# Blocks of 128 rows made of two 64-row pieces of any two of 64 small experts

## The reference

```python
logits = jnp.einsum('bsh,he->bse', hidden_states.astype(jnp.float32), router_w)
affinity = jax.nn.sigmoid(logits)
top_scores, top_idx = jax.lax.top_k(affinity, K)          # K = 8 of E = 64
gate_out = jnp.einsum('bsh,ehi->bsei', hidden_states, expert_gate_k)   # h 256, i 128
up_out = jnp.einsum('bsh,ehi->bsei', hidden_states, expert_up_k)
expert_act = jax.nn.silu(gate_out) * up_out
routed = jnp.einsum('bsei,eih->bsh', expert_act * router_mask[..., None], expert_down_k)
```

## Time and profile before

| | us |
|---|---|
| median of 3 runs | 2946.24 (2945.65 to 2948.47) |
| the profiled execution | 2942.13 |
| its span, first to last instruction | 2940.4 |
| the blocks stage, from TensorE's first transpose to ScalarE's last copy of y | 1425.9 to 1729.8 |

### The profile page before, as it was taken

How to read it: one execution, slowest core, us unless ns; L and a number is a source line. 1 busy time by engine, 2 the same in 40 slices (tenths; PEclk the granted TensorE clock), 3 DMA queues, 4 the chain that set the end, 5 groups by cost and what they waited for, 6 DMA issues and landing times. The chain is left out here.

```text
span 2940.4 us, 58466 instructions
## 1 busy us (share of the span) xinstructions
PE 2799.0 (95%) x17307; PEld 1928.4 (66%) x17308; DVE 1525.5 (52%) x4471; ACT 1029.3 (35%) x2709; POOL 926.6 (32%) x1784
## 2 busy tenths in 40 slices
PE   7999999999999999995999988999999999999798
PEld 5777676677777677674788855556565665656475
DVE  4445555555555555554655545555555555554343
ACT  1433334333433434332333323343333433334121
POOL 0012222122112222113455535534344343430332
PEclk9999999999999999997999999999999999999899
DMA  6000000000000000002588871100001000000350
GB/s 224 8 7 7 7 7 7 7 7 2 7 5 7 7 7 7 7 2 93 157 264 260 197 166 30 40 24 21 21 25 34 24 21 21 28 17 4 122 187 20
DMA packets 89488, 154.78 MB, mean 53 GB/s; under 512 B 19266, under 2 KB 64335, under 8 KB 87888
## 3 DMA queue, kind: packets, MB, share of 16 engines
q1 hardware_dynamic: 39952, 85.60, 9.0%
q0 software_dynamic: 22320, 45.30, 6.5%
q10 hardware_dynamic: 27152, 23.09, 2.3%
HBM read 122.86 MB, written 31.99 MB: 53 GB/s over the span
## 5 line engine op out<-in xcount | busy, mean ns | idle before, releaser
L927 PE MATMUL psG<-W,ctxT 128*125 128x512 f32 (+2 forms) x896 | 408.6, 599 | 4.2 <-DVE v L2435 4.2
L1520 ACT ACTIVATE probs<-psG,nmax 112x375 f32<-112x375 f32 (+1 forms) x512 | 317.0, 620 | 252.0 <-DVE nmax L1891 252.0
L921 PE MATMUL psG<-ctxT,W 128*128 128x375 f32 (+1 forms) x1024 | 386.8, 525 | 2.3 <-ACT ctxT L1718 1.2
L1891 DVE TENSOR_REDUCE nmax<-psG 112x1 f32<-112x375 f32 (+1 forms) x512 | 284.9, 601 | 120.5 <-PE psG L869 116.0
L886 PEld LDWEIGHTS psT<-ident,probs 112*125 112x125 f32 (+2 forms) x1792 | 201.3, 167 | 157.5 <-ACT probs L1520 110.6
L921 PEld LDWEIGHTS psG<-ctxT,W 128*128 128x128 f32 x1024 | 188.9, 189 | 163.1 <-issue 106.5
L915 PEld LDWEIGHTS psG<-hT,W 128*128 128x128 f32 x2304 | 268.5, 194 | 24.9 <-ACT hT L1547 16.2
L915 PE MATMUL psG<-hT,W 128*128 128x112 f32 x2304 | 278.9, 280 | 3.2 <-ACT hT L1547 3.2
L927 PEld LDWEIGHTS psG<-W,ctxT 128*125 128x125 f32 (+2 forms) x896 | 159.6, 187 | 177.9 <-issue 170.8
L886 PE MATMUL psT<-ident,probs 112*125 112x112 f32 (+2 forms) x1792 | 248.5, 276 | 20.2 <-ACT probs L1520 16.3
L869 PE MATMUL psG<-kT,qT 64*112 64x375 f32 (+1 forms) x1024 | 243.9, 563 | 1.1 <-DVE v L2435 0.6
(11 more groups left out here) (374 smaller groups left out, 4190.8 us busy)
## 6 DMA issues: line engine op xcount, KB each, us to landing
W<-in_ew SPq DMA_DIRECT2D x64, 384.0 KB, 4.6
expert_rows<-W ACTq DMA_DIRECT2D x176, 128.0 KB
W<-in_ew SPq DMA_DIRECT2D x8, 2048.0 KB, 8.9
ctxT<-in_ctxT SPq DMA_DIRECT2D x16, 375.0 KB, 3.1
kT<-in_ctx SPq DMA_DIRECT2D x16, 375.0 KB
W<-in_eb SPq DMA_DIRECT2D x8, 640.0 KB, 10.9
normed_rows<-hrow SPq DMA_DIRECT2D x32, 112.0 KB, 1.9
W<-normed_rows,ids POOLq DMA_INDIRECT x176
```

What stands on the lines that cost most here:

```text
L921: mm = nc.tensor.matmul(bank[:, 0:n], wt[:, c, n0 + j * P:n0 + (j + 1) * P], src[:, c, 0:n], start=(c == 0), stop=(c == DC - 1))
L927: mm = nc.tensor.matmul(bank[0:kn, 0:512], src[:, c, k0:k0 + kn], wt[:, c, n0 + half * 512:n0 + (half + 1) * 512], start=(c == 0), stop=(c ...
L1520: nc.scalar.activation(probs[:, 2 * (s % 2) + i, 0:keys], psG[0:T, score_banks(s)[i], 0:keys], ACT.Exp, bias=nmax[:, h:h + 1], accum_out=r ...
L1891: nc.vector.tensor_reduce(nmax[:, 2 * s + i:2 * s + i + 1], psG[0:T, score_banks(s)[i], 0:keys], AXX, ALU.max, negate=True).then_inc(max_r ...
```

## The change

For the 64 small experts a block is made of two pieces of 64 rows, and the two pieces may belong to any two experts. The eight large experts keep blocks of 128.

- `Experts` gets a piece size. There are at most 14336/64 + 64 = 288 pieces, so 144 blocks. `brow` has 288 entries, one for each piece, and the tables count in pieces (add 63, shift by 6). The id rows of 64 numbers are fetched by four indirect loads. `lrow` is halved to blocks at the end.
- TensorE multiplies each half of the rows with its own weights: the upper piece (rows 0 to 63) with the weights in the ring, the lower piece (rows 64 to 127) with weights at a fixed place, `lower[i]`, one of eight. Each product becomes two, with 64 stationary columns each, into PSUM partitions 0 to 63 and 64 to 127.
- The weights of the lower piece are copied there from the ring for every block: ScalarE copies gate and up (512 elements of each partition), VectorE copies down (256). Each reads the rank of the lower piece from `brow` into a register, computes the place in the ring, and waits until that rank is loaded. This is so too where both pieces are of one expert.
- The pipelines of TensorE, ScalarE and VectorE go in pairs of blocks. On TensorE: transposes of blocks i and i+1, transposes of h of i-4 and i-3, gate and up of i-2 and i-1, down of i-4 and i-3. `xT0` gets four buffers for two.
- Some semaphores are shared between the two mixtures, and `brow` moves to the storage of `hT1` and `hT2`.

```diff
-        self.NBLK = -(-(TOK * topk // P + experts) // 4) * 4
+        self.NBLK = -(-(TOK * topk // piece + experts) * piece // P // 4) * 4
+        self.NP = self.NBLK * P // piece
...
-        L0E, L1E = Experts(0, 64, 8, 8, 768), Experts(1, 8, 1, 4, 5376)
+        L0E, L1E = Experts(0, 64, 8, 8, 768, 64), Experts(1, 8, 1, 4, 5376, P)
...
+        lower = [W[:, 17152 + 768 * i:17920 + 768 * i] for i in range(5)]
+        lower += [flat[:, 512 + 768 * i:1280 + 768 * i] for i in range(3)]
...
             for i, n in enumerate((P, L0E.NBLK - P)):
-                nc.gpsimd.indirect_dma_start(
-                    out=idrow[0:n, i, :], out_offset=None, in_=rows0,
-                    in_offset=bass.IndirectOffsetOnAxis(ap=gcol[0:n, i:i + 1], axis=0)).then_inc(S0.idrow_in, 16)
+                for k in range(2):
+                    nc.gpsimd.indirect_dma_start(
+                        out=idrow[0:n, i, half * k:half * k + half], out_offset=None, in_=rows0,
+                        in_offset=bass.IndirectOffsetOnAxis(ap=gcol[0:n, 2 * i + k:2 * i + k + 1],
+                                                            axis=0)).then_inc(S0.idrow_in, 16)
...
+                def pair(turn, i, lo, hi=0):
+
                     if hi < 1:
...
+                        for k in range(i, i + 2):
+                            j = At(turn, k, UNROLL)
+                            pe.wait_ge(s.xg_in[j.m], 16 * (j.turn + 1))
+                            for c in range(DC):
+                                mm = nc.tensor.transpose(psG[:, j.m2, c * P:(c + 1) * P], xg0[:, j.m, c * P:(c + 1) * P],
+                                                         ident[:])
+                            mm.then_inc(s.xT_full, 1)
+                    if lo >= 2:
+                        for k in range(i - 4, i - 2):
+                            j = At(turn, k, UNROLL)
+                            pe.wait_ge(s.h_done, j.j + 1)
+                            nc.tensor.transpose(psT[:, j.m2, 0:P], hh[:, j.m2, :], ident[:]).then_inc(s.hT_full, 1)
                     if lo >= 1 and hi < 2:
...
+                        for k in range(i - 2, i):
+                            j = At(turn, k, UNROLL)
+                            pe.wait_ge(s.xT_done, j.j + 1)
+                            pe.wait_ge(s.loaded, pe.snap(first[k % 4], min_val=0, max_val=l.E - 1) + 1)
+                            pe.wait_ge(s.up_copied, j.j + 1)
+                            for c in range(DC):
+                                for h in range(2):
+                                    mm = nc.tensor.matmul(psG[half * h:half * h + half, 2 + j.m2, 0:256],
+                                                          xT0[:, j.m, c, half * h:half * h + half], weights(c, k, h),
+                                                          start=(c == 0), stop=(c == DC - 1))
+                            mm.then_inc(s.gu_full, 1)
...
+                            pe.wait_ge(s.hT_done, j.j + 1)
+                            pe.wait_ge(s.down_copied, j.j + 1)
+                            if not (isinstance(j.j, int) and j.j < 2):
+                                pe.wait_ge(s.y_done, j.j - 1)
+                            for h in range(2):
+                                mm = nc.tensor.matmul(psO[half * h:half * h + half, j.m2, 0:D],
+                                                      hhT[:, j.m2, half * h:half * h + half], weights(2, k, h),
+                                                      start=True, stop=True)
+                            mm.then_inc(s.y_full, 1)
...
+                def copy_up(j, i):
+
+                    act.reg_load(loaded_rank, brow[0:1, bass.ds(2 * j + 1, 1)])
+                    act.reg_alu(rank, loaded_rank, 0, ALU.max)
+                    act.reg_alu(slot, rank, l.R - 1, ALU.bitwise_and)
+                    act.reg_alu(slot, slot, l.wsize, ALU.mult)
+                    act.wait_ge(s.loaded, act.snap(rank, min_val=0, max_val=l.E - 1) + 1)
+                    at = act.snap(slot, min_val=0, max_val=(l.R - 1) * l.wsize)
+                    nc.scalar.activation(lower[i][:, 0:512], W[:, bass.ds(RING + at, 512)],
+                                         ACT.Copy).then_inc(s.up_copied, 1)
+
+                def pair(turn, i, lo, hi=0):
+                    if hi < 1:
+                        for k in range(i, i + 2):
+                            copy_up(At(turn, k, UNROLL).j, k)
                     if lo >= 1 and hi < 2:
...
+                        for k in range(i - 2, i):
+                            j = At(turn, k, UNROLL)
+                            act.wait_ge(s.gu_full, j.j + 1)
+                            nc.scalar.activation(sg[:, j.m2, :], psG[:, 2 + j.m2, 0:P], ACT.Silu).then_inc(s.sg_done, 1)
+                    if lo >= 2:
+                        for k in range(i - 4, i - 2):
+                            j = At(turn, k, UNROLL)
+                            act.wait_ge(s.y_full, j.j + 2)
+                            act.wait_ge(s.y_stored[j.m], 16 * j.turn + 16)
+                            nc.scalar.activation(ysb0[:, j.m, :], psO[:, j.m2, 0:D], ACT.Copy).then_inc(s.y_done, 1)
+                            act.wait_ge(s.y_done, j.j + 1)
+                            store(l, s, j)
```

More of the change, by code:

```diff
@@ L1206, in tables1 @@
                 pe.wait_ge(s.slots_ok, B)
[L1207 removed]
+                nc.tensor.matmul(psG[0:E, 0, 0:1], cum1, ones[0:T, 0:1], start=True, stop=True).then_inc(S0.counts_full, 1)
                 pe.wait_ge(s.blocks_ok, 1)
@@ L1240, in blocks0 @@
                 pe.sem_inc(s.y_full, 1)
[L1242 to L1248, removed]
-                    if hi < 1:
[L1250 to L1255, removed]
-                    if lo >= 1 and hi < 2:
[L1257 to L1274, removed]
@@ new lines, in blocks0, with weights @@
+                half = l.piece
+                first = [pe.alloc_register(f"upper_rank{i}") for i in range(4)]
+                slots = [pe.alloc_register(f"ring_slot{i}") for i in range(UNROLL)]
+                def weights(c, i, k):
+                    if k:
+                        return lower[i % UNROLL][:, 256 * c:256 * c + 256]
+                    slot = pe.snap(slots[i % UNROLL], min_val=0, max_val=(l.R - 1) * l.wsize)
+                    return W[:, bass.ds(RING + slot + 256 * c, 256)]
@@ L1275, in step @@
                     if hi < 1:
-                        load_rank(At(turn, i, UNROLL).j, i, l)
-                for i in range(UNROLL):
-                    step(0, i, i)
+                        for k in range(i, i + 2):
+                            load_upper(At(turn, k, UNROLL).j, k)
+                for i in range(0, UNROLL, 2):
+                    pair(0, i, i // 2)
                 with pe.Fori(1, l.NBLK // UNROLL) as turn:
-                    for i in range(UNROLL):
-                        step(turn, i, 3)
@@ L1283, in blocks0 @@
-                for i in range(3):
-                    step(l.NBLK // UNROLL, i, 3, i + 1)
+                    for i in range(0, UNROLL, 2):
+                        pair(turn, i, 2)
+                for i in range(0, 4, 2):
+                    pair(l.NBLK // UNROLL, i, 2, i // 2 + 1)
             def blocks1(l, s):
@@ L1664, in blocks0 @@
[L1664 to L1670, removed]
+                act.wait_ge(s.tables, 1)
+                loaded_rank = act.alloc_register("loaded_rank_act")
+                rank, slot = act.alloc_register("lower_rank_act"), act.alloc_register("lower_slot_act")
@@ L1672, in blocks1 @@
+                for i in range(0, UNROLL, 2):
+                    pair(0, i, i // 2)
+                with act.Fori(1, l.NBLK // UNROLL) as turn:
+                    for i in range(0, UNROLL, 2):
+                        pair(turn, i, 2)
+                for i in range(0, 4, 2):
+                    pair(l.NBLK // UNROLL, i, 2, i // 2 + 1)
             def blocks1(l, s):
@@ L2280, in blocks0 @@
-                for i in range(4):
-                    step(0, i, i)
-                with dve.Fori(1, l.NBLK // 4) as turn:
-                    for i in range(4):
-                        step(turn, i, 4)
-                for i in range(2):
-                    step(l.NBLK // 4, i, 4, i + 1)
+                dve.wait_ge(s.tables, 1)
+                loaded_rank = dve.alloc_register("loaded_rank_dve")
+                rank, slot = dve.alloc_register("lower_rank_dve"), dve.alloc_register("lower_slot_dve")
@@ new lines, in pair @@
+                def pair(turn, i, lo, hi=0):
+                    if hi < 1:
+                        for k in range(i, i + 2):
+                            j = At(turn, k, UNROLL)
+                            dve.wait_ge(s.xT_full, j.j + 1)
+                            nc.vector.tensor_copy(xT0[:, j.m], psG[:, j.m2, 0:DC * P].rearrange(
+                                "p (c t) -> p c t", c=DC)).then_inc(s.xT_done, 1)
+                    if lo >= 2:
+                        for k in range(i - 4, i - 2):
```

(19 more changed lines are left out.)

164 lines of the change are left out of this document (86 added, 78 removed).

## The result

| | before | after |
|---|---|---|
| median | 2946.91 us (2945.65 to 2948.47, 4 runs) | 2971.59 us (2969.18 to 2973.50, 4 runs) |
| the profiled execution; its span | 2942.13; 2940.4 | 2972.38; 2970.6 |
| ScalarE's last copy of y ends at | 1729.83 | 1756.18 |

The ratio is 1.0085, with an interval from 1.0072 to 1.0097: 25 us slower.

What follows compares the result with a forecast made beforehand. TensorE bounds the kernel before; after the change ScalarE's 4.30 us lap would bound the small experts' stage. Stage +7.7 and tables +3.0 give +10.7 us, a median of 2957 us from 2946.24, range 2926 to 2990.

Steps and rivals of the forecast that it cites:

- the plain lap: ScalarE's work for one pair of blocks, with every wait on others satisfied: 4.30 us.
- Part 1 and 3: Small experts: 144 blocks for 176 save TensorE 53 us; VectorE with its weight copies needs 3.4 to 3.7 us a pair.
- Part 2: Products in halves on TensorE: halves run side by side, 0.25 us for mode changes, 3.51 us a pair against 3.32.
- Part 4: Weight copies on ScalarE: its lap becomes 4.30 us a pair against TensorE's 3.51, so ScalarE becomes the bound.
- register part: ScalarE's rank read, address and wait value ahead of each weight copy: 0.72 us, twice a pair, the first exposed behind a store.
- weights come late: Rival: copies or products wait for expert weights to arrive, each us of wait one of the end; chance 0.03.
- The Trainium skill's rule on SBUF copies: ScalarE's SBUF copies: latency exposed between instructions would remove the 0.10 us overlap, result 7 us later; one copy 0.61 us.
- Stage in sum: Small experts' stage: second SiLU at 1432.4, 69 laps of 4.30, end at 1737.5 against 1729.8, so +7.7 us.
- Part 5: Tables and id rows: two more indirect loads +2.5 us, wider comparisons and one more shift +0.5.
- TensorE as the bound: Rival: ScalarE's reads hide and the lap falls to TensorE's 3.51 us, giving 2902 us; chance 0.24.
- The halves in turns: Rival: TensorE's half products run one after another, 6.1 us a pair, +135 us, 3081; chance 0.05.
- a falling clock: Rival: TensorE, partly idle, is held at 1.2 GHz, 6.9 us a pair, +190 us, 3136; chance 0.04.

Runs made afterwards that it cites:

- e1: Changed kernel with ScalarE's weight copies taken from a fixed place, without rank read, register operations or load wait (wrong weights): 2913.11 us, 0.9901 of the kernel before.
- e7: Changed kernel with one y copy and one store for a pair, and ScalarE's ranks read a pair ahead: 2927.01 us, 0.9948 of the kernel before.
- e9: Changed kernel with TensorE's reads of the next pair's ranks between gate/up and down instead of behind down: 3108.37 us, 1.0092 of the kernel before.
- e12: Kernel of e7 with TensorE's rank reads moved between the gate/up and down products: 2954.03 us, 1.0044 of the kernel before.
- e11: Kernel of e7 run again, on one chip with e12: 2925.66 us, 0.9946 of the kernel before.
- e4: Changed kernel with y of a pair copied by one instruction and stored by one DMA: 2934.74 us, 0.9976 of the kernel before.
- e5: Changed kernel with ScalarE's two rank reads for the next pair placed behind this pair's weight copies: 2935.98 us, 0.9990 of the kernel before.

## Why the prediction was right, and its size too small

The sign, the bound and the plain lap were right; the forecast was +10.7 us and the medians say +24.7.

- **Part 1 and 3.** 72 pairs ran. VectorE did not set the pace in the changed kernel: in each pair it waits 1.5 us for SiLU (65.8 us in 44). At 3.70 us a pair (e1) it still kept up, within my 3.4 to 3.7. The row of 0.28 that I took for a copy from SBUF is a product which reads PSUM too; the copies took 0.34 to 0.35 on the average.
- **Part 2, TensorE's pair of 3.51.** Its halves run side by side. In the timeline of TensorE two passes start within 0.01 us, and the next two 0.21 later:

```profile
1551.93 0.38 PE L1298 MATMUL psG<-W 128*64 x1
1551.94 0.38 PE L1298 MATMUL psG<-kT,W 128*64 128x256 f32 x1
1552.14 0.38 PE L1298 MATMUL psG<-W 128*64 x1
1552.15 0.38 PE L1298 MATMUL psG<-kT,W 128*64 128x256 f32 x1
```

  The first half product starts at 1551.67 and the second pair at 1551.93, so 0.05 more than a pitch, where 0.25 was charged for going in and out of the halves. What the part left out is TensorE's own reads, two ahead of each pair with nothing queued behind the down products: 27.2 us of 200, and 39.6 in e7. It did not cost the changed kernel anything (e9). I took it for what stops e7 at 3.92 instead of 3.51; but with these reads moved the kernel was slower (e12), so what holds e7 there is not shown.
- **Part 4, the lap of 4.30.** The plain laps are 4.31 (only the first two, at 4.19 and 4.18, are shorter). The register part behind a store was 0.79 (read 0.27, the rest 0.52) and the hidden one 0.77 from copy to copy, each for 0.72; the stores were as charged; the two SiLUs with their wait values took 0.32 for 0.43. That 4.31 lies so near is in part luck: these two errors cancel. But 69 laps, from the first copy of y at 1437.64 to the one at 1749.83, took 312.2 us, 4.52 each, where 296.7 stood in the sum. **This is the term that was too small:** the lap was summed with every read at its median and the branch at next to nothing. Of the 15.5 us too few, 2.8 are the plain lap (4.31 for 4.27 without the branch). Another 4.3 are the loop's branch: the 16 laps that hold it are 0.40 longer, 0.31 of that between the store's issue (end 1552.69) and the weight copy and 0.08 ahead of the second copy of y, where I charged 0.03 a lap. The last 8.4 are long reads: the 138 reads of ScalarE's sequencer in these laps took 8.4 us more in sum than at 0.275 each, and in all but three laps the excess over 4.31, the branch aside, is that of the lap's two reads within 0.05 us.
  The rows of line 1703 name the arrival of weights (L463) ahead of ten copies:

```profile
  issue: 101.7, 122
  SPq L463: 11.7, 10
```

  But these ten waited no longer than their own reads explain. A copy behind a store has 1.30 us of idle time, a second one 0.15, with reads of 0.27. Two of the named waits:

```profile
1485.51 0.63 ACT L1703 ACTIVATE W<-W 128x512 f32 x1 [1.41 <-SPq L463]
1576.10 0.63 ACT L1703 ACTIVATE W<-W 128x512 f32 x1 [1.31 <-SPq L463]
```

  The read ahead of the first took 0.38, that of the second 0.29; in none of the ten are more than 0.03 us left over. So "weights come late" did not happen: in all ten the load's signal came 0.07 to 0.93 us before the copy started.
  One sum of the range is incomplete: its lower end, 3.86, takes the register part's bound and not the copy's, with which it would be 3.73.
- **The Trainium skill's rule on SBUF copies.** The 0.10 of overlap was kept: a weight copy ends at 1559.53, and the SiLU behind it starts at 1559.43. In e11 two SBUF copies stand in a queue:

```profile
1557.49 1.15 ACT L1707 ACTIVATE W<-W 128x512 f32 x2 [0.97 <-ACT W L1725]
```

  Two copies in 1.15 us, where one is 0.63: the second starts 0.10 before the end of the first. The Trainium skill, page "VectorE: DVE Perf Modes", section on the TRN2 errata, says that SBUF latency stays exposed between instructions; for ScalarE's copies this trace does not agree, and its length for one (an estimate of 0.61) does.
- **Stage in sum.** The second SiLU ended at 1434.4, where 1432.4 and the tables' 3.0 give 1435.4: 1.0 early. From the first transpose to that SiLU it took 4.5 us where before took 5.1; the two blocks transposed ahead, charged with 1.4, cost nothing. From there to the last y came 321.7 for 305.1: the 15.5 of the laps, and 1.1 in the first lap and the drain. At the stage's end that is +26.3 for +10.7. Behind the stage the profiled execution took 3.8 us more than that of before (1214.4 for 1210.6), which this account leaves open.
- **Part 5.** The wait for the id rows is 1.5 us longer, where I took 2.5; the tables add 1.5 for 0.5 (0.45 of it was there before their first instruction on VectorE). Some 1.2 us more (the conversion of the id rows to floats comes 2.7 later, the first transpose 4.0) are lost in the shared expert, at a granted clock of 0.91 from 1405 to 1425, where before had 1.00; the cause is open.
- **The rivals.** TensorE as the bound needed a lap of 3.5; it came near only with ScalarE's reads away (e1). The halves in turns and a falling clock did not happen: the granted clock was 1.00 with TensorE waiting in every pair.

## What to carry to other kernels

Cut work on the engine that sets the end only after summing the lap of the engine that takes over, its sequencer included: here two parts of 0.8 us, reads and address arithmetic, of which one lay bare behind a store, helped to turn fewer blocks, worth 1.66 to 1.97 us each, into a loss. Then add to that best lap what single laps cost beyond it (the branch, the reads that are longer than their median); here it was 5% of the lap and more than the whole forecast. Where such a loss is found, first take the register reads and stores off the queue that decides: with one store for two blocks and ScalarE's ranks read a pair ahead, e7 and e11 beat both kernels, at 0.9948 and 0.9946 of the one before.

## What the runs showed of the hardware

- A sequencer's read of one integer from SBUF takes 0.27 (ScalarE) to 0.30 us (TensorE, VectorE) at its shortest, and up to 1.17 (e12). With the shorter laps of e11, 125 of 305 were over 0.5 us, against 24 of 264 after. Each of them, and of SyncE's that were as long, overlaps in time with a read of another engine's sequencer (136 in e11, 29 after). Overlap alone doesn't make a read long: 140 of the 250 that took under 0.33 us in e11 overlap too. The gains of e4 and e5, 32 and 30 us, became 39 together; these long reads are a likely cause, and no run took them away.
- A loop's branch made ScalarE's lap 0.40 us longer; the branch instruction itself is 0.045.
- A copy of 512 elements for one of 256 twice, from PSUM, took 0.60 us for 0.77, and the issue of a store of two blocks 0.38 for 0.34.
- The granted clock stayed 1.00 for 200 us with TensorE idle 0.6 us by modelled ends in every pair of 4.55.
